# Three parts instead of four in the middle stage of a transformer block with experts, and three shared tiles moved behind the experts

## The reference

```
h = _layernorm(x) * (1 + cb) + sb
logits = h @ w_router.T; probs = softmax(logits); keep the two largest of 8
acc = shared network (512 wide, gelu) of h
    + sum over the two kept experts: gate * (gelu(h @ W1[e].T + b1[e]) @ W2[e].T + b2[e])
x = x + gb * SCALE * acc
```

## Time and profile before

| what | us |
|---|---|
| median of 3 runs | 683.43 |
| the profiled execution's own time | 682.79 |
| its span, first to last instruction | 680.9 |
| busy in it: PE, DVE, ACT, POOL | 594.7, 428.7, 315.2, 350.4 |
| training steps end, last block starts | about 353 |
| first, last indirect transfer of the dispatch issued | 388.73, 489.79 |
| first PE work of the experts, last | 497.93, 647.4 |
| first sum on PE, end of the span | 659.54, 680.9 |

### The profile page before, as it was taken

The page is one execution under the profiler, slowest core; times in us unless marked ns, Lnnn a source line. Parts: engine busy times, 40 slices in busy tenths (PEclk is TensorE's granted clock), DMA queues, the critical chain, the costliest instruction groups (busy, mean ns, idle before and its releaser), DMA issues. The chain is left out here.

```text
span 680.9 us, 14547 instructions
## 1 busy us (share of the span) xinstructions
PE 594.7 (87%) x4322; PEld 519.4 (76%) x4322; DVE 428.7 (63%) x1766; ACT 315.2 (46%) x996; POOL 350.4 (51%) x556
## 2 busy tenths in 40 slices
PE   1459999999999999999965898899399999999927
PEld 1339999999999999999843776677289989999912
DVE  2846888888888888888847767374044545445406
ACT  1455666666666666666513342353044444434300
POOL 1025666666666666666526386575615455454520
PEclk9999999999999999999978787889799999999969
DMA  9059900000000000000000011111737678787457
GB/s 213 6 230 414 410 32 1 1 0 0 0 0 0 0 0 0 0 0 1 2 0 1 4 49 37 40 45 38 221 88 215 217 212 239 210 230 227 145 183 210
DMA packets 42739, 66.76 MB, mean 98 GB/s; under 512 B 7394, under 2 KB 30692, under 8 KB 42692
## 3 DMA queue, kind: packets, MB, share of 16 engines
q1 hardware_dynamic: 31908, 52.74, 25.0%
q0 software_dynamic: 4544, 9.45, 3.8%
q10 hardware_dynamic: 6240, 4.00, 2.2%
HBM read 36.25 MB, written 29.92 MB: 97 GB/s over the span
## 5 line engine op out<-in xcount | busy, mean ns | idle before, releaser
L1770 POOL DMA_INDIRECT ys<-yo,dst x78 | 74.6, 957 | 87.7 <-DVE yo L1685 71.8
L1473 ACT ACTIVATE hid<-bank,slab 128x256 f32<-128x256 f32 x156 | 63.5, 474 | 87.9 <-PE bank L1364 79.5
L1762 POOL DMA_INDIRECT xs<-hrow,slot_i x64 | 68.9, 1077 | 35.1 <-issue 23.8
L1375 PEld LDWEIGHTS bank<-slab,hid 128*128 128x128 f32 x624 | 75.6, 192 | 2.0
L1364 PE MATMUL bank<-hg,slab 128*128 128x256 f32 x312 | 74.7, 382 | 1.7 <-issue 0.7
L1375 PE MATMUL bank<-slab,hid 128*128 128x128 f32 x624 | 75.8, 275 | 0.0
L1364 PEld LDWEIGHTS bank<-hg,slab 128*128 128x128 f32 x312 | 56.2, 190 | 9.5 <-issue 2.5
L1465 ACT ACTIVATE hs<-bank,sb 128x256 f32<-128x256 f32 x64 | 26.2, 474 | 62.7 <-PE bank L1330 42.0
L1346 PE MATMUL bank<-sw,hs 128*128 128x128 f32 x256 | 37.7, 304 | 9.9 <-ACT hs L1465 7.4
L1346 PEld LDWEIGHTS bank<-sw,hs 128*128 128x128 f32 x256 | 34.1, 212 | 16.1 <-ACT hs L1465 10.5
L1668 DVE SCALAR_TENSOR_TENSOR row<-xt,etab 128x2 f32<-128x2 f32 x39 | 8.6, 220 | 58.1 <-DMA ys<-yo,dst 48.5
(11 more groups left out here) (313 smaller groups left out, 1813.7 us busy)
## 6 DMA issues: line engine op xcount, KB each, us to landing
slab<-in_slabs_dram SPq DMA_DIRECT2D x39, 578.0 KB
xs<-fill SPq DMA_DIRECT2D x34, 528.0 KB
xt<-xs SPq DMA_DIRECT2D x39, 132.0 KB
xr<-in_L_attn_x_dram SPq DMA_DIRECT2D x8, 256.0 KB, 8.9
yg<-ys SPq DMA_DIRECT2D x4, 512.0 KB, 8.8
yg<-ys ACTq DMA_DIRECT2D x4, 512.0 KB, 9.7
ys<-yo,dst POOLq DMA_INDIRECT x78
xs<-hrow,slot_i POOLq DMA_INDIRECT x64
```

The lines of the kernel that those rows point to most:

```text
L1375: mm = pe.matmul(bank[4 + j % 2][:, s * D:(s + 1) * D], hid[j % 2][:, n, s * P:(s + 1) * P], slab[j % RW][:, F + n * P:F + (n + 1) * P], s ...
L1473: nc.scalar.activation(hid[j % 2][:, n, :], e_half(j, n), ACT.Gelu_apprx_tanh, bias=slab[j % RW][:, 2 * F + n:2 * F + n + 1]).then_inc(e_x, 1)
L1762: pool.indirect_dma_start(out=xs[:, :], out_offset=bass.IndirectOffsetOnAxis(ap=slot_i[:, i, c:c + 1], axis=0), in_=hrow[:, c, :], in_offs ...
L1770: pool.indirect_dma_start(out=ys[:, :], out_offset=bass.IndirectOffsetOnAxis(ap=dst[r][:, s:s + 1], axis=0), in_=yo[r][:, s, :], in_offset ...
```

## The change

The middle stage is cut into parts of 8, 12 and 12 chunks (`PARTS` are group numbers). ACT writes plain normalised rows `xn`, which PE transposes; the modulation is applied twice: by ACT on the transposed side (`modulate`), for the router and the networks, and by DVE to the rows that are dispatched (`rows`). POOL keeps only the bias of groups 0 and 1; for the others PE adds it with one more matmul before `result`. DVE adds all results. Nearly all small DVE instructions are written as SCALAR_TENSOR_TENSOR, with a different 1/deviation iteration. Three shared tiles (13 to 15) stand behind the experts. All eight loads of `yg` are issued by SP.

```diff
-SG = 8
-NSG = CH // SG
-GSG = SG // GRP
-TSG = SG // SUB
+PARTS = ((0, 2), (2, 5), (5, 8))
+LONGEST = 12
+EARLY = 2
+LAST = 3
...
                 def turn(g):
-                    pe.wait_ge(placed, (g + 1) * GRP)
+                    pe.wait_ge(xn_ready, g + 1)
...
-                        t = pe.transpose(bank[4 + g % 2][:, j * P:(j + 1) * P], hrow[:, g * GRP + j, 0:D], ident[:, :])
+                        t = pe.transpose(bank[4 + g % 2][:, j * P:(j + 1) * P], xn[:, place(g) + j, :], ident[:, :])
...
+                    if g >= EARLY:
+                        pe.matmul(bank[2 + g % 2][:, :], ones[:, :], diag[:, :].unsqueeze(1).broadcast_to([P, GRP, D]),
+                                  start=True, stop=False, skip_group_check=True)
...
+                    if t == N_SH - LAST:
+                        pe.wait_ge(e_x, FT * N_TILES)
...
+                def normalise(g):
+                    k = part(g)
+                    act.wait_ge(r_ready, k + 1)
+                    if k:
+                        act.wait_ge(turned, PARTS[k][0])
+                        act.wait_ge(scaled, PARTS[k][0])
+                    for j in range(GRP):
+                        c = g * GRP + j
+                        n = nc.scalar.activation(xn[:, place(g) + j, :], xr[:, c, :], ACT.Identity,
+                                                 bias=nmr[:, c:c + 1], scale=rstd[:, c:c + 1])
+                    n.then_inc(xn_ready, 1)
+
+                def modulate(g):
+                    act.wait_ge(turned, g + 1)
+                    src = bank[4 + g % 2][:, :].rearrange("p (c t) -> p c t", c=GRP)
+                    for b in range(B):
+                        rows = slice(b * STEPS, (b + 1) * STEPS)
+                        m = nc.scalar.activation(hT[:, g * GRP:(g + 1) * GRP, rows], src[:, :, rows], ACT.Identity,
+                                                 bias=modT[:, 2, b:b + 1], scale=modT[:, 3, b:b + 1])
+                    m.then_inc(hT_ready, 1)
...
+                def rows(g):
+                    dve.wait_ge(xn_ready, g + 1)
+                    hx = hrow[:, g * GRP:(g + 1) * GRP, 0:D]
+                    dve.tensor_tensor(hx, xn[:, place(g):place(g) + GRP, :], cbrow[:, :].unsqueeze(1).broadcast_to([P, GRP, D]),
+                                      ALU.mult).then_inc(scaled, 1)
+                    dve.wait_ge(scaled, g + 1)
+                    dve.tensor_tensor(hx, hx, sbrow[:, :].unsqueeze(1).broadcast_to([P, GRP, D]), ALU.add).then_inc(placed, 1)
...
                 pool.wait_ge(gab_ready, 1)
-                for g in range(4):
+                for g in range(EARLY):
                     add_bias(g)
-                for g in range(3):
-                    add_result(g)
-                for g in range(4, NG):
-                    add_bias(g)
-                for g in range(3, BY_POOL):
-                    add_result(g)
-                for k in range(NSG):
+                for k in range(len(PARTS)):
                     dispatch(k)
```

More of the change, by code:

```diff
@@ L1225, in program, with chunks, part, place @@
             ys_v = ys[0:2 * B * S, :].rearrange("(c p k) d -> p c (k d)", p=P, k=2)
+            def chunks(k):
+                a, z = PARTS[k]
+                return a * GRP, z * GRP
+            def part(g):
+                return sum(g >= z for a, z in PARTS)
+            def place(g):
+                return (g - PARTS[part(g)][0]) * GRP
             def all_scattered(eng):
@@ L1268, in _ @@
                 all_scattered(sp)
-                for g in range(0, NG, 2):
+                for g in range(NG):
                     load(sp, g)
@@ L1434, in _ @@
                     e_down(j)
+                up(N_SH - LAST)
+                for t in range(N_SH - LAST + 1, N_SH):
+                    up(t)
+                    down(t - 1)
+                down(N_SH - 1)
                 for g in range(NG):
@@ L1499, in _ @@
                     e_gelu(j)
-                all_scattered(act)
-                for g in range(1, NG, 2):
-                    load(act, g)
+                for t in range(N_SH - LAST, N_SH):
+                    gelu(t)
                 for g in range(1, NG, 2):
@@ L1566, in normalise @@
[L1566 to L1574 removed]
+                    both_of(tmp[:, cs], rstd[:, cs], 1.0, rstd[:, cs], ALU.mult, ALU.mult)
@@ L1620, in slots @@
+                    dve.tensor_copy(slot_i[:, :, c0:c1], slotf[:, :, 0:n]).then_inc(slot_ready, 1)
                     dve.wait_ge(sum_step, k + 1)
@@ L1692, in _, with x1 @@
                 dve.tensor_tensor(gab[:, :], bank[6][:, 0:D], gate[:, 0, :], ALU.mult).then_inc(gab_ready, 1)
-                times_gate(0)
-                times_gate(1)
+                def x1(g):
+                    times_gate(g)
+                    add_result(g)
+                x1(0)
                 statistics(0)
-                times_gate(2)
+                x1(1)
                 statistics(1)
                 spread(0)
-                normalise(0)
+                x1(2)
+                rows(0)
+                statistics(2)
+                rows(1)
                 times_gate(3)
+                choose(0)
                 times_gate(4)
-                choose(0)
-                times_gate(5)
                 gates(0)
                 slots(0)
+                add_result(3)
+                statistics(3)
+                add_result(4)
+                statistics(4)
+                spread(1)
+                x1(5)
                 times_gate(6)
+                rows(2)
+                rows(3)
+                rows(4)
                 times_gate(7)
+                choose(1)
+                post(0)
+                gates(1)
+                slots(1)
+                post(1)
+                statistics(5)
                 add_result(6)
+                statistics(6)
                 add_result(7)
-                for k in range(1, NSG):
-                    t = (k - 1) * TSG
-                    for g in range(k * GSG, (k + 1) * GSG):
-                        statistics(g)
-                    spread(k)
-                    normalise(k)
-                    post(t)
-                    post(t + 1)
-                    choose(k)
-                    post(t + 2)
-                    gates(k)
-                    slots(k)
-                    post(t + 3)
+                statistics(7)
+                spread(2)
+                post(2)
+                rows(5)
+                rows(6)
+                rows(7)
+                post(3)
+                choose(2)
+                post(4)
+                gates(2)
+                slots(2)
                 tables()
-                for t in range(N_SH - TSG, N_SH):
+                for t in range(5, N_SH - LAST):
                     post(t)
@@ L1733, in _ @@
                     e_post(j)
+                for t in range(N_SH - LAST, N_SH):
+                    post(t)
                 dve.wait_ge(sh_ready, N_SH)
```

327 lines of the change are left out of this document (183 added, 144 removed).

## The result

The change takes **704.17 us** (median of 4 runs, 701.09 to 704.77), the kernel before 685.51 us on the same chip (median of 4, 681.53 to 688.29): ratio **1.0268, interval 1.0201 to 1.0335**. It is slower; the forecast was 666 us, with a range to 681. The profiled execution took 703.93 us (span 702.1), against 682.79 (span 680.9).

The account below looks back on a forecast made before the run. POOL's dispatch of 64 indirect transfers, 102 us, was taken to bound the experts' start. An earlier start (-16.4 us) and a shorter end (-1.2) summed to -17.6, giving 666 us; range 654 to 681.

Parts of the forecast that it names:

- the holds: Middle stage: what PE finishes during a batch of POOL's transfers is not seen by others until about 2 us after it.
- the chain of batches: POOL's three dispatch batches, timed from 382.0 to a last transfer at 472.4 instead of 490.75: -18.4 us.
- my own rule: In POOL's batches, a hold begins near the 13th transfer and ends about 2 us behind the batch.
- the last hold takes the whole batch: Rival, last dispatch batch: hold from the slabs, 446 to 474.5, experts at 496.5, 681 us in all; chance 0.12.
- a fetch of code was queued behind the slabs: Before the experts: skill-based reading of ACT's 17.25 us wait as a delayed code fetch; sum 661.
- Part 1: Second batch's preparation: ACT 8 us, route ends 398, choose 401.3, places held to 404.3, batch starts at 406.5.
- The first part: Start up to the first row numbers: 381.1 against 387.76, -6.7 us, bounds 378 and 385.
- ACT's two last silu, the exponentials and a table load of 1.28 end at 379.3: First part, behind choose at 376.7: ACT ends at 379.3, gates and slots 1.7 more, row numbers at 381.1.
- The rule of the Trainium skill on the shared port pair: Dispatch beside DVE's two-input instructions: if it applies to transfers, 3.8 us per part instead of 0.5, sum 672.
- The end: After the last expert tile: three tiles add 1.4, sums at clock 1.00 take 13.7 instead of 16.3; -1.2 us.
- bulk transfers hold PE's messages at the end: Rival, tiles 13 to 15 and sums: yg loads delay PE's answers, +8 at the end, 690 us; chance 0.07.
- my 481.5: Start of the experts: first expert work on PE at 481.5 against 497.93, -16.4 us, including 13 lost to a hold.

Follow-up runs that it names:

- e16_same: The change unaltered, run again on another block's chip where the kernel before takes 686.04 us: ratio 1.0314.
- e18_busy: The change with five POOL memsets of 1.40 us inside the batches, repeated on the chip of the unaltered change's rerun: ratio 0.9852 to the kernel before.
- e13_short: The change with five short POOL memsets of 128x32 inside the batches, on the chip without holds: ratio 1.0045 to the kernel before.
- e10_busy: The change with a POOL memset of 128x1536 at five places inside the batches, no landing waited for: 675.68 us, 0.9855 of the kernel before.
- e12_slabs_late: The change with SP's first five slabs issued only when the last dispatch transfer has landed: ratio 1.0355 to the kernel before.
- e4_halves: The change with first-choice rows in batches of 8, 12 and 12 transfers, then all 32 second-choice transfers: 715.17 us, 1.0307 of the kernel before.
- e7_paced_down: The change with POOL's landing waits inside batches, plus down(0) on PE moved behind route(1): ratio 0.9851 to the kernel before.
- e9_bias_pool: The change with POOL's landing waits inside batches, and all eight bias additions on POOL instead of PE's six bias matmuls: ratio 0.9927 to the kernel before.
- e15_before_busy: The kernel before with a 1.40-us POOL memset in the middle of each batch of 16, on the chip without holds: ratio 1.0035.
- e3_paced: The change with POOL waiting at five places inside the batches until all transfers issued so far have landed: 680.23 us, 0.9799 of the kernel before.
- e6_tail_paced: The kernel before with three shared tiles behind the experts, yg loads from SP and a landing wait mid-batch: ratio 0.9932.

## Why the prediction was wrong

| step, us of the span | forecast | the change | the change again (`e16_same`) | with breaks (`e18_busy`, same chip as `e16_same`) |
|---|---|---|---|---|
| first transfer starts | 382.0 | 386.84 | 386.29 | 386.46 |
| second batch starts | 406.5 | 420.80 | 425.41 | 416.46 |
| third batch starts | 441.6 | 471.28 | 476.30 | 453.62 |
| last transfer ends | 472.4 | 501.36 | 506.33 | 486.63 |
| experts start | 481.5 | 520.89 | 524.83 | 491.09 |

**The step that failed** is the one on the holds in "the chain of batches": "a hold from the 13th transfer (422) to 437.3 + 2.1 = 439.4 catches its `places`". I had read the hold as something that begins at a count and costs what is left of a batch behind `places`. It caught the transposes, four steps earlier, held them from 440.06 to 454.73, and then `modulate`, `route` (5.13 us at the half clock), the table load, `choose` and `places` were still to be done one by one, with POOL idle. The last two columns give the holds' price on one chip: 9.0 us at the second batch, 13.7 more up to the third (50.9 against 37.2), 11.1 more up to the experts (48.5 against 37.5), 33.7 in all; the first trace less `e18_busy` gives 4.3, 13.3, 12.1 and 29.8. Part 2 was also later than I had it without any hold: in `e13_short` its row numbers are there 30 us after the second batch starts (446.95 less 416.75), not 23.5, and in the change its transposes start 18.2 us after that start. By then the 13th transfer (436.44) was under way, so even my own rule would have caught the transposes; I had put `places` alone in its way. The end of a hold I had right: 2.9 us behind the last transfer (454.73 against 451.84), where I took 2. The Trainium skill ("Perfetto Trace Analysis", "DMA Instruction — SWDGE (GPSIMD)") says that such a row ends when the last descriptor is written and not when the data has moved; the distance fits that, but by `e10_busy` it is not the landing that must be waited for.

**The last batch.** My rival "the last hold takes the whole batch" (0.12) came close to what happened: ACT gets answers at 490.42, 496.68 and 505.31 only, PE ends its tiles at 520.14. Its price of 681 was too low because it stood on a third batch at 441.6. I had made the slabs its cause; `e12_slabs_late` shows that a hold of this length comes without them. With that falls the case in which a fetch of code was queued behind the slabs. That the code came late for another reason is not borne out either: no instruction packet stands in the two stretches under `e4_halves`.

**Part 1, 10 us without any hold** (406.5 forecast, 416.46 with breaks): the second, smaller error. In the first trace ACT's share was to take 8 us and took 15.8, from 391.85 to 407.63: 12 `normalise` in 4.73, `gelu(1)`, then 3.89 us for PE, which had `down(0)` in front of `turn(2)` at a clock of 0.60, then 12 `modulate`. And `places(1)` was to follow `choose` at once; it stood behind `up(2)` and `down(1)`, at 417.81 against 413.2. I had counted the steps of the part and not what PE had queued between them. `e7_paced_down` shows that moving one of these pieces only moves the wait.

**The first part**: -1.9 us instead of -6.7, just outside the bound of 385 for the row numbers (385.86). `spread(0)` at 2.8 us and the logits (375.40 against 373.6) were near enough; the failing term is "ACT's two last silu, the exponentials and a table load of 1.28 end at 379.3". They ended at 384.11, since `result(4)`, 3.8 us at the half clock, and `hidden(6)` stood on PE in front of them. `e9_bias_pool` acquits the bias matmuls. (The sum itself has a slip of 0.2: 372.8 + 1.0 is 373.8, not 373.6.)

**Right:** no transfer over 1.5 us (longest 1.47); three of the second batch took 1.23 us, beside DVE's six additions and multiplications of 128x512, so 0.8 us of POOL's time where I had 0.5. The rule of the Trainium skill on the shared port pair ("SBUF — State Buffer", "SBUF: two separate sides"), read so that a transfer counts as an operation that reads SBUF, would have had 3.8; this trace is against that reading. The end: -1.8 us against -1.2, sums in 14.0 us against 13.7, all at 1.00. The rival "bulk transfers hold PE's messages at the end" did not happen.

**Luck:** that the experts start at 483.42 in `e13_short`, 2 us from my 481.5. Two errors cancel there: the last transfer ends 6.6 us later than forecast (478.99 against 472.4), and the hold by which I had PE lose 13 us is absent. That the change could be slower had a chance of 0.07, but for a cause at the end that did not appear.

**What the change is worth without holds** is nothing that can be measured: `e13_short` has 1.0045 (1.0002 to 1.0089), beside a kernel before that takes 666.73 us on that chip. From the experts' start to the end of the span it is 182.0 us in `e15_before_busy` and 183.0 in the first trace of before, so what before gains there lies in front of the experts, where the holds were. My gains in front of the experts rested on a comparison with a trace that had holds of its own.

What a hold is stays open. The runs show that it comes with unbroken transfers and how it is broken, and that PE itself can crawl in it; they do not show what slows PE or keeps its messages back, nor why one chip of those used here has none. On the short breaks there is one comparison, on one chip.

**The best version** is the change with the breaks: 0.9855 (`e10_busy`) and 0.9852 (`e18_busy`) of before, and 0.9799 in the form that waits for landings (`e3_paced`), whose interval overlaps theirs. All three are faster than before, none of them by 2% for certain; five breaks cost POOL 5 x 1.37 us (a gap of 1.67 us instead of 0.30), and on the chip without holds this kernel was not run.

## What to carry to other kernels

When an engine's answers come late in a trace and the consumer was idle, the length of the wait is no constant to be carried into the new order: ask which step of a serial chain it will hit, since everything behind that step is paid again. A rule read off four cases (begins at the 13th, ends 2 us behind the batch) needs one run that breaks it before a plan is built on it; here one memset would have done. And a step's place in its engine's queue is part of its cost: count what stands in front of `places`, not only the steps that it depends on.

## What the runs showed of the hardware

- While POOL issued indirect transfers without a break, PE's work reached ACT and DVE late, in every block but one: ACT was idle for up to 26 us (44 transfers in a row, `e4_halves`).
- In such a stretch PE itself could slow down: 16 matmuls of one `down` took 23.6 us instead of 2.05 to 3.78, one every 2.80 us (`e4_halves`), with nothing in the profile to wait for and no instruction packet on the DMA queues.
- A pause of POOL every 8 transfers (a gap of 1.6 to 1.7 us) brings the time down, whether POOL waits for landings, 0.9799, or runs a memset, 0.9855 and 0.9852; waits of ACT of up to 9.40 us are left. A memset of 0.14 to 0.15 us does not, 1.0364.
- On one chip none of this appears, and the kernel before runs in 666.73 us instead of 685 to 694.
- A wait for landings after 8 transfers costs POOL 1.6 to 1.7 us when nothing else is under way, and up to 5.3 us beside the slabs (`e6_tail_paced`).
